# Relative attention in a six-layer decoder: a batch's closing normalisation one step later, a turn of probabilities and the divisions moved, waits split by bank

## The reference

```
dist = clip(idx[None, :] - idx[:, None], -64, 64) + 64
pe_k, pe_v = rel_emb_k[dist], rel_emb_v[dist]
q, k, v = split(x @ W_qkv + b_qkv);  q = q / sqrt(16)
score = einsum('bhqd,bhkd->bhqk', q, k) + einsum('bhqd,qkd->bhqk', q, pe_k)
attn = softmax(score, axis=-1)
ctx = einsum('bhqk,bhkd->bhqd', attn, v) + einsum('bhqk,qkd->bhqd', attn, pe_v)
x = layernorm(x + ctx @ W_out + b_out)
```

## Time and profile before

| what | value |
|---|---|
| median of 3 runs | 1798.02 us (1796.23 to 1798.17) |
| profiled execution, its own time | 1808.23 us |
| its span | 1806.5 us |
| relative attention, first scores to last | 638 to 1010 us |
| PE busy | 1618.8 us, 90% |
| DVE busy | 1171.4 us, 65% |
| ACT busy | 676.3 us, 37% |
| POOL busy | 316.2 us, 18% |
| share of the chain that ended last: PE | 60% |

### The profile page before, as it was taken

One profiled execution on the slowest core, in us unless ns is written; L12 is line 12 of the kernel. 1 busy time (PEld: TensorE's weight loads), 2 busy tenths in 40 slices (PEclk: granted clock), 3 DMA queues, 4 the chain that ended last, 5 costly groups with the idle time before them and its releaser, 6 DMA issues.

```text
span 1806.5 us, 38627 instructions
## 1 busy us (share of the span) xinstructions
PE 1618.8 (90%) x14760; PEld 1267.3 (70%) x14760; DVE 1171.4 (65%) x3823; ACT 676.3 (37%) x1426; POOL 316.2 (18%) x335
## 2 busy tenths in 40 slices
PE   6799996899997879899978788997999999999997
PEld 4677775666665757677756657775887888788876
DVE  3555664455563756566656447449888889889884
ACT  3333331245556446565545444132222222222210
POOL 1443434200001200000122006410010001000100
PEclk9899998999999989999989887899999999999999
DMA  3100000000111279999999951320000000000000
GB/s 127 47 19 19 19 13 19 12 19 25 31 55 49 82 285 328 315 321 321 336 322 331 303 178 35 123 94 2 2 13 2 13 8 7 13 2 13 6 3 13
DMA packets 98358, 177.29 MB, mean 98 GB/s; under 512 B 16128, under 2 KB 82688, under 8 KB 93440
## 3 DMA queue, kind: packets, MB, share of 16 engines
q1 hardware_dynamic: 98176, 174.82, 28.1%
HBM read 92.88 MB, written 81.79 MB: 97 GB/s over the span
## 4 chain that ended last, share of the span: by engine, by line
PE 60%; issue 14%; DVE 10%; ACT 4%; DMA 4%; POOL 3%; DVEq 2%; POOLq 2%; SPq 0%; ACTq 0%
PE bank L104 20%; PE bank L2995 10%; PE bank L112 5%; PE bank L2955 3%; PE bank L2982 3%; DMA rel_p_rows<-rel_probs 2%; PE bank L970 2%; PE bank L1746 2%; PE bank L986 1%; PE bank L97 1%; ACT rel_probs L1547 1%; PE bank L1780 1%; PE bank L1002 1%; PE bank L1767 1%; DVE first_shared L422 1%
## 5 line engine op out<-in xcount | busy, mean ns | idle before, releaser
L104 PE MATMUL bank<-per_xT,per_down 128*128 128x256 f32 x1024 | 250.7, 390 | 2.3 <-ACT per_xT L2674 1.6
L2995 PE MATMUL bank<-per_up,per_act_w 128*128 128x256 f32 x1024 | 242.7, 383 | 0.0
L2995 PEld LDWEIGHTS bank<-per_up,per_act_w 128*128 128x128 f32 x1024 | 195.5, 192 | 27.0
L2681 ACT ACTIVATE per_act_w<-bank 128x512 f32<-128x512 f32 x128 | 76.3, 597 | 364.4 <-PE bank L104 329.8
L104 PEld LDWEIGHTS bank<-per_xT,per_down 128*128 128x128 f32 x1024 | 190.4, 192 | 29.9 <-issue 2.7
L1547 ACT ACTIVATE rel_probs<-later_shared,rel_low 128x256 f32<-128x256 f32 x256 | 114.9, 519 | 32.1 <-DVE rel_low L1630 32.1
L1630 DVE CUSTOM_DVE_ANT_0 later_shared<-bank,later_shared 128x256 f32<-128x256 f32 x256 | 92.9, 419 | 40.0 <-PE bank L1746 19.0
L922 DVE TENSOR_REDUCE xat_mx<-bank 128x2 f32<-128x512 f32 x128 | 79.4, 684 | 34.9 <-PE bank L970 34.9
L2661 POOL TENSOR_TENSOR per_sim<-per_sim,per_best_i 128x512 f32<-128x512 f32 x32 | 41.9, 1329 | 332.5 <-DVE per_sim L2799 332.5
L104 PE MATMUL bank<-ret_x2T,ret_w_in 128*128 128x256 f32 x384 | 93.0, 399 | 7.5 <-issue 7.5
L1780 PE MATMUL bank<-ident,rel_probs 128*128 128x128 f32 x512 | 88.0, 308 | 1.1 <-ACT rel_pT L1555 1.1
(11 more groups left out here) (365 smaller groups left out, 3171.3 us busy)
## 6 DMA issues: line engine op xcount, KB each, us to landing
rel_qr_rows<-later_shared SPq DMA_DIRECT2D x32, 1024.0 KB, 7.8
rel_p_rows<-rel_probs SPq DMA_DIRECT2D x32, 1024.0 KB, 9.8
later_shared<-rel_qr_rows SPq DMA_DIRECT2D x64, 384.0 KB, 4.7
rel_by_dist<-rel_p_rows SPq DMA_DIRECT2D x64, 384.0 KB, 5.2
per_down<-in_per_down SPq DMA_DIRECT2D x1, 4096.0 KB, 12.4
per_up<-in_per_up SPq DMA_DIRECT2D x1, 4096.0 KB, 13.3
ret_xin<-in_x SPq DMA_DIRECT2D x8, 256.0 KB, 2.9
xat_cT<-in_contextT SPq DMA_DIRECT2D x8, 256.0 KB, 3.0
```

What stands on the lines that cost most here:

```text
L104: last = pe.matmul(dst, wt[:, c], src[:, c, :], start=c == 0, stop=c == DC - 1)
L2681: nc.scalar.activation(act_w[m % 2][:, 2 * k:2 * k + 2, :], tiles(bank[3 + k % 2]), ACT.Gelu_apprx_tanh).then_inc(gelu_ready, 1)
L2995: last = pe.matmul(tiles(bank[7])[:, t, :], act_w[n % 2][:, k, t * P:t * P + P], up[:, k, :], start=k == 0, stop=k == COLS - 1)
```

## The change

Six edits, all in the fourth layer:

- A batch is normalised on DVE and stored by SP two steps after its output projection instead of one (`end_of`); the last two batches keep their step. POOL's root keeps its step.
- On SP the store (and the taking of a new x) stands behind the step's two stores of rows instead of ahead of them.
- DVE's divisions stand in the gather's own step, behind the copies of the table and ahead of the far sums, instead of at the start of the next step; each half waits for its own bank.
- PE's third turn of probabilities stands behind the table and the second turn of distances, directly ahead of the batch's jobs, in steps that have such jobs.
- `all_read` becomes `bank_read(s, r)`, which waits for one bank, ahead of the first use of that bank.
- `oU_turned` is counted per half.

```
+    def end_of(s):
+        last = out_of(s - 1)
+        return last if last is not None and last >= nb - 2 else out_of(s - 2) if out_of(s - 2) != nb - 2 else None
...
-            if (b := out_of(s - 1)) is not None:
-                sp.wait_ge(y_ready, b + 1)
-                sp.dma_start(batch_of(x_out, b), yout[:, b % 2]).then_inc(stored[b % 2], 16)
...
                 sp.dma_start(p_rows[U % 2], probs[:, U % 2, :, REACH:REACH + ROW]
                              .rearrange("p h k e -> p h (k e)")).then_inc(p_saved[U % 2], 16)
+            if (b := end_of(s)) is not None:
+                sp.wait_ge(y_ready, b + 1)
+                sp.dma_start(batch_of(x_out, b), yout[:, b % 2]).then_inc(stored[b % 2], 16)
+                if b + XS < nb:
+                    sp.wait_ge(x_used, b + 1)
+                    take_x(sp, b + XS)
...
-            if (b := gather_of(s - 1)) is not None:
-                dve.wait_ge(oU_turned, b + 1)
...
-            if (b := out_of(s - 1)) is not None:
+            if (b := end_of(s)) is not None:
                 dve.wait_ge(rstd, b + 1)
                 normalise(dve, yout[:, b % 2], yout[:, b % 2], mv[:, b % 2], rs[:, b % 2])[-1].then_inc(y_ready, 1)
...
+            if (b := gather_of(s)) is not None:
+                if b >= 2:
+                    dve.wait_ge(o_turned, b - 1)
+                for t in range(TT):
+                    dve.wait_ge(oU_turned, TT * b + t + 1)
...
             if (U := unit(s - 1)) is not None:
                 far_sums(U)
...
-        def all_read(s):
+        def bank_read(s, r):
             if (n := min(s + 4, UNITS)) >= 1:
-                pe.wait_ge(qr_act, 2 * n)
-                pe.wait_ge(qr_dve, 2 * n)
+                pe.wait_ge((qr_act, qr_dve)[r // 2], 2 * (n - 1) + r % 2 + 1)
             if (n := min(s + 2, UNITS)) >= 1:
-                pe.wait_ge(summed_ready, 4 * n)
+                pe.wait_ge(summed_ready, 4 * (n - 1) + r + 1)
...
-            if (U := turn_of(s)) is not None:
+            jobs = any(of(s) is not None for of in (x_turn_of, gather_of, project_of, out_of))
+            if (U := turn_of(s)) is not None and not jobs:
                 turn_probs(U, 2)
...
             if (U := dist_of(s)) is not None:
                 turn_dist(U, 1)
+            if (U := turn_of(s)) is not None and jobs:
+                turn_probs(U, 2)
```

More of the change, by code:

```diff
@@ L1471, in sync @@
                         .then_inc(dist_loaded[U % 3], 16)
-            if (b := out_of(s - 1)) is not None:
-                sp.wait_ge(y_ready, b + 1)
-                sp.dma_start(batch_of(x_out, b), yout[:, b % 2]).then_inc(stored[b % 2], 16)
-                if b + XS < nb:
-                    sp.wait_ge(x_used, b + 1)
-                    take_x(sp, b + XS)
             if (U := table_of(s)) is not None:
@@ L1597, in scalar @@
                 if b >= 2 and U % GROUPS == 0:
-                    act.wait_ge(oU_turned, b - 1)
+                    act.wait_ge(oU_turned, TT * (b - 1))
                 nc.scalar.activation(oU[:, b % 2, U % GROUPS], tiles(bank[7])[:, U % 2], ACT.Copy)\
@@ L1653, in vector @@
                                 bank[2][:].rearrange("p (a e) -> p a e", e=HD)).then_inc(v_ready, 1)
-            if (b := gather_of(s - 1)) is not None:
-                dve.wait_ge(oU_turned, b + 1)
-                if b >= 2:
-                    dve.wait_ge(o_turned, b - 1)
-                for t in range(TT):
-                    parts = bank[1 + t][:].rearrange("p (h e) -> p h e", e=VW)
-                    dve.reciprocal(rsum[:, t], parts[:, :, HD])
-                    dve.drain()
-                    last = dve.tensor_tensor(o[:, b % 2, t].rearrange("p (h e) -> p h e", e=HD),
-                                             parts[:, :, 0:HD], over(rsum[:, t], HD), ALU.mult)
-                last.then_inc(o_ready, 1)
             if (b := out_of(s - 1)) is not None:
@@ L1698, in vector @@
                                     .rearrange("p (t k) -> p t k", t=TT)).then_inc(qr_dve, 1)
+            if (b := gather_of(s)) is not None:
[3 more added lines that the diff above has]
+                    dve.wait_ge(oU_turned, TT * b + t + 1)
+                    parts = bank[1 + t][:].rearrange("p (h e) -> p h e", e=VW)
+                    dve.reciprocal(rsum[:, t], parts[:, :, HD])
+                    dve.drain()
+                    last = dve.tensor_tensor(o[:, b % 2, t].rearrange("p (h e) -> p h e", e=HD),
+                                             parts[:, :, 0:HD], over(rsum[:, t], HD), ALU.mult)
+                last.then_inc(o_ready, 1)
             if (U := unit(s - 1)) is not None:
@@ L1845, in tensor @@
                 turn_dist(U, 1)
+            if (U := turn_of(s)) is not None and jobs:
+                turn_probs(U, 2)
             if (b := x_turn_of(s)) is not None:
-                all_read(s)
+                bank_read(s, 0)
                 pe.wait_ge(x_loaded[b % XS], 16 * (b // XS + 1))
@@ L1850, in tensor @@
                 if b == 0:
+                    bank_read(s, 3)
                     constants()
             if (b := gather_of(s)) is not None:
-                all_read(s)
                 pe.wait_ge(oU_ready, GROUPS * (b + 1))
                 for t in range(TT):
+                    bank_read(s, 1 + t)
                     for g in range(GROUPS):
@@ L1858, in tensor @@
                                             ident[:])
-                last.then_inc(oU_turned, 1)
+                    last.then_inc(oU_turned, 1)
             if (b := project_of(s)) is not None:
-                all_read(s)
                 pe.wait_ge(xT_ready, b + 1)
@@ L1865, in tensor @@
                 for k, wt, done in ((0, wq, q_mm), (1, wk, k_mm)):
+                    bank_read(s, k)
                     for g in range(DC):
@@ L1870, in tensor @@
                     pe.wait_ge(wv_loaded, 16)
+                bank_read(s, 2)
                 by_token(pe, tiles(bank[2]), xT[:, b % 2], wv).then_inc(v_mm, 1)
             if (b := o_turn_of(s)) is not None:
-                all_read(s)
+                bank_read(s, 3)
                 pe.wait_ge(o_ready, b + 1)
```

## The result

| what | before | changed |
|---|---|---|
| median of 20 runs each | 1798.1 us (1787.6 to 1810.6) | 1785.64 us (1775.26 to 1796.53) |
| ratio of the two | 1 | 0.9915, 95% interval 0.9896 to 0.9933 |
| profiled execution, its own time; its span | 1808.23 us; 1806.5 us | 1796.53 us; 1794.7 us |

Against the 1798.02 us of before the ratio is 1782.7 us: 15.3 us faster (12.0 to 18.7), where 8.5 was forecast. The two medians alone give a ratio of 0.9931, or 12.5 us, which lies inside the interval; 1785.64 us would be inside the range. So the size of the gain is known to a few us only.

What follows compares the result with a forecast made beforehand. SP's loop of stores waiting for landings was taken to set the pace, not PE. Terms 2.0 (store) + 4.7 (stall) + 1.2 (divisions) + 0.6 (layer's end) = 8.5 us, from 1798.0 to 1789.5 us; range 1783 to 1796.

Steps and rivals of the forecast that it cites:

- SP's loop: Middle of the layer: probabilities' store landing plus 1.47 us on SP makes the 11.30 us period and sets the pace, not PE.
- PE's waits count: Rival, full batches: PE bounds without the profiler, some of 3.01 us per batch counts; 1783.5 us, up to 1771.4; chance 0.08.
- The stall: Steps 22 and 26, DVE and SP waiting for POOL's root: removing it gains 4.7 us over nine periods, ends 0 and 10.0.
- nine periods near 106 us: Sign of being right: the stretch from 906.04 to 1017.15, 111.11 us before, falls to about 106 us.
- The store out of the loop: SP, batches 0 to 2: the batch's store behind the stores of rows gains 2.0 us, ends 0 and 2.8.
- the transfers give it back: Rival: transfer engines are full, so what is issued sooner lands no sooner; 3.0 us gained, 1795.0 us; chance 0.17.
- The normalisation a step later: DVE, steps 3: its 0.74 us costs nothing there, and the root is ready when DVE comes, at 923 or later.
- Third turn, waits bank by bank: PE, middle of the layer: worth zero, since PE has slack against the loop and job waits won are lost at the table.
- Divisions 1.2 at the layer's end: Last batch: PE no longer stands for the divided heads; 1.2 us gained, between 0 and 1.35.
- the slower rival: Steps 3: far sums queued behind the divisions make PE wait, 1.8 us per batch; 1805.9 us; chance 0.05.
- SP at the layer's end: Batch 5's store leaves the place ahead of the last probabilities' store: 0.58 us gained, summed as 0.6.
- middle batches shorter by 2 us or more: Sign of being wrong: middle batches that much shorter would mean PE is the bound; hardly shorter than 46 us was expected.

Runs made afterwards that it cites:

- e4: Kernel before with only the third turn, the waits bank by bank and the divisions changed; normalisation and store as before: 1795.96 us, ratio 0.9977.
- e1: Kernel before with only the batch's store (and taking of x) moved behind SP's two stores of rows, same step: 1797.74 us, ratio 0.9978.
- e11: Changed kernel with SP's distance reads also behind the step's two stores, second run of that kernel: 1779.13 us, ratio 0.9885 to before.
- e2: Kernel before with only the normalisation and the batch's store one step later, store still ahead of the stores of rows: 1790.49 us, ratio 0.9945.
- e3: Kernel before with normalisation and store one step later and the store behind the stores of rows, nothing else: 1784.68 us, ratio 0.9915.
- e5: Changed kernel with PE's third turn of probabilities put back ahead of the table: 1789.45 us, ratio 0.9922 to before.
- e6: Changed kernel with the divisions put back at the start of the next step: 1790.94 us, ratio 0.9920 to before.
- e8: Kernel before with only SP's mLSTM context reads and stores of centred values one step earlier: 1793.06 us, ratio 0.9939.

## Why the prediction was wrong in size and right in its mechanism

**SP's loop is the bound of the middle: right.** Parts aimed at PE gave nothing there (e4), the store out of the loop did (e1), and opening the loop did more (e11). The rival that PE's waits count is out for this kernel, apart from single periods like that of e1 in step 21, and true of the next one.

**The stall: the term that failed.** It stood at 4.7 us, from the assumption that the transfers would go back to the middle's share of 0.95. They went to 0.98 to 1.00 in the seven profiles without the stall that have the distance reads in their old place (both of the changed kernel, e2, e3, e5, e6, e8); the sign "nine periods near 106 us" failed with it. The mean of their nine periods is 100.1 us (98.0 to 101.6), that of the four with it (both of before, e1, e4) 108.1 (105.9 to 111.1): 8.0 us, or by the first two profiles alone 10.0, of which some 2 are a profile of before at the long end. I had that case as the upper end of the term (10.0 at a share of 1.0) and gave it too little. 0.95 was the share of a loop that waits for landings; in this stretch the mLSTM's reads and stores lie between, and it is likely that they fill the rest, but no run here takes them out. The stretch now runs at 355 GB/s at a share of 0.99, that of e3 at 366 at 1.00, and e11's at 362; the 402 GB/s that I set against such a rate held for 7.6 us. The Trainium skill's 358 GB/s at the HBM side of a core (DMA: Bandwidth & Descriptors, section Bandwidth) gave at most 10.8 us by the estimate in the prediction. The long stretches come within 2.3% of it, on both sides. The same section gives it as the share of a core while both cores of a pair stream, and has 425 GB/s for one core alone, so for this kernel on one core the agreement may be chance. What the runs do show is that a rate held over 100 us, or the upper end of the share, was the better measure for this term.

**The store out of the loop: too small.** It stood at 2.0 us (0 to 2.8) for batches 0 to 2, by SP's issue time alone. The periods that end in steps 10, 14 and 18 are 12.7 us on the mean of the four profiles with the store in its old place (both of before, e4, e8), and 11.2 on that of the six with it behind (both of the changed kernel, e1, e3, e5, e6): 1.5 us per store, 4.5 in all. Units 4 to 16, which hold the first two of the three, are 4.3 us shorter (141.5 and 137.2), 3.3 of it in those two periods. The size is a mean over profiles: single periods of these kernels with the store behind run from 10.4 to 13.0 us. What I left out is likely the store's own bytes, 0.26 MB, ahead of the two stores on the same engines: at 342 GB/s 0.8 us, beside the 0.58 of issue. I counted them as work that must be done wherever it stands; behind the stores it is done beside the latency of the next step's reads. No run here separates issue from bytes. The rival that the transfers give it back is out: the landing stayed at 10.1 us and the share of the middle batch rose from 0.95 to 0.98.

**The normalisation a step later: right.** It runs at 917.55 without a wait, and SP's stores of the steps 3 do not wait for data. The margin was thin, 1.4 us from the root, and the times behind it were not those of the estimate: POOL began at 910.94 instead of 917.31, and DVE was there at 917.55 instead of 923 or later.

**Third turn, waits bank by bank: zero in the middle, right.** The sign I looked for, a longer row of the table, is not shown: the table's wait is 4.8 us instead of 2.7, but 5.7 in the second profile of before. **Divisions 1.2 at the layer's end: right**, 1.26, and gone again in e6. PE waits for the far sums once, at the layer's end, in the kernel before too (0.86 and 1.29 us before, 2.12 and 1.16 in the changed one). Behind it stand the last distances, for which DVE waits, and not the divisions, so the slower rival had no hold.

**SP at the layer's end** stood at 0.6, and is seen in the last period before unit 31's store: 9.1 us on the mean of the four profiles with the store ahead (9.0 to 9.2), 8.2 on that of the six with it behind (8.0 to 8.5). This 0.9 us is part of the 8.0 for units 22 to 31. Behind that store nothing is gained but the divisions: the shorter wait for the reloaded x is made up by the longer one for the last distances. What else differs to the mLSTM goes with the granted clock, as in e4: the hundred PE instructions behind the turn of distances take 11.8 us at 0.74 and 10.9 at 0.79 (before), 10.4 at 0.85 and 9.0 at 1.00 (changed).

The parts as the profiles' means show them, 4.5 + 8.0 + 1.3, make 13.8 us, within the 12.0 to 18.7 of the ratio. By these parts the time would be 1784.2 us, inside the range; what misses to the 15.3 of the ratio is less than its interval and has no cause shown. A marker was badly chosen too: "middle batches shorter by 2 us or more" should have meant that PE was the bound, and they were shorter by up to 2.8 (44.20 us) for the loop's own sake.

## What to carry to other kernels

A queue that issues a store only after the store before it has landed is a loop whose length is a latency; look for it where issues follow one another at issue distance, and take out of it whatever needs not be in it (that the bytes count as well as the instruction is likely here, not shown). A transfer share below 1 in such a loop says little of the room: measure the rate where the queue is kept full. Where two bounds lie close, test an edit again after the other bound has been moved: in the profiles the moves on PE were worth nothing here and some 8 us behind one more edit on SP.

## What was not expected of the hardware

The mLSTM's part is the same code in all profiles and takes 110.3 to 125.7 us. Its length goes with its mean granted clock: 110.8 us at 0.88, 114.6 at 0.85 (twice), 119.1 at 0.79, 125.7 at 0.71. The rows of e3 and of e4 in which PE does the same 552 instructions:

```profile
1037.75:1148.51 110.76, 94.20 (x552) 76.47 (x552) 65.52 (x203) 40.08 (x98) 55.41 (x61) 0.88 0.32 117
```

```profile
1047.94:1170.73 122.79, 109.41 (x552) 88.84 (x552) 64.66 (x202) 40.25 (x98) 55.00 (x61) 0.75 0.29 108
```

In it the clock goes between its two levels, 2.4 and 1.2 GHz, with 27 us at the lower one in e3, 61 in e4 and 72 in the changed kernel's profile. It differs between two profiles of one kernel as well (0.71 and 0.78 for the changed one), so none of it is put down to an edit here. It is as large as the effects sought: 15 us between the ends, and the span of one profile says less than its stretches.
